# The mixing stage of a two-layer convolution kernel: another split of the nine depthwise taps over TensorE, VectorE and ScalarE, with the products in a ring of 7 slots

## The reference, cut to what matters

```python
# x: (8, 128, 256, 256) float32
def layer0(x):                                # x := x + this, of groupnorm(x)
    ll, lh, hl, hh = haar_dwt(x)              # four images of 128 x 128
    h = concat([ll, lh, hl, hh], axis=1)      # 512 channels
    h = gelu(batchnorm(conv1x1(h, w_c1, b_c1)))      # to 128 channels
    res = h
    o = dwconv3x3(h, dw_w, dw_b)              # nine taps for each channel
    o = layernorm_chw(o, gn_g, gn_b)          # one mean and variance for each image
    o = conv1x1(gelu(conv1x1(o, pw1_w, pw1_b)), pw2_w, pw2_b)
    h = o + res
    h = gelu(batchnorm(conv1x1(h, w_c2, b_c2)))      # to 512 channels
    return haar_idwt(h)
def layer1(x):                                # x := x + this, of groupnorm(x)
    return blur4x4(x)                         # the same 4 x 4 taps for all channels
```

## Time and profile before

| | |
|---|---|
| median of 3 runs | 5690.55 us (5673.53 to 5690.85) |
| the profiled execution's own time | 5687.8 us |
| its span | 5685.9 us |
| busy over the span: PE, DVE, ACT, POOL | 92%, 77%, 65%, 36% |
| mixing stage in the span | about 1236 to 2583 us |
| granted TensorE clock, mean over the span | 0.968 |

### The profile page before, as it was taken

One profiled execution on the slowest core, in us unless ns is written; L12 is line 12 of the kernel. 1 busy time (PEld: TensorE's weight loads), 2 busy tenths in 40 slices (PEclk: granted clock), 3 DMA queues, 4 the chain that ended last, 5 costly groups with the idle time before them and its releaser, 6 DMA issues. The chain is left out here.

```text
span 5685.9 us, 67157 instructions
## 1 busy us (share of the span) xinstructions
PE 5206.1 (92%) x18136; PEld 3152.4 (55%) x18136; DVE 4380.2 (77%) x5325; ACT 3721.4 (65%) x5012; POOL 2068.4 (36%) x1397
## 2 busy tenths in 40 slices
PE   2888888986999999996689999999999999999999
PEld 1333333332555555563256666666666766666677
DVE  8555555428999999957988888888888888888833
ACT  0333333346778777754678788787887877878744
POOL 0000000028777777730023333333333333333354
PEclk9999999998999999998899999999999999999999
DMA  9999999842333333326999999999999999999986
GB/s 368 374 372 380 369 380 378 345 143 71 108 108 112 104 108 108 108 83 226 326 381 403 393 401 398 390 402 384 398 392 384 394 384 397 399 384 395 400 292 228
DMA packets 829594, 1729.83 MB, mean 304 GB/s; under 512 B 50064, under 2 KB 587152, under 8 KB 718608
## 3 DMA queue, kind: packets, MB, share of 16 engines
q1 hardware_dynamic: 755472, 1389.81, 66.9%
q10 hardware_dynamic: 73728, 335.58, 14.4%
HBM read 1050.95 MB, written 674.23 MB: 303 GB/s over the span
## 5 line engine op out<-in xcount | busy, mean ns | idle before, releaser
L1080 POOL TENSOR_TENSOR y_lo<-y_centred_tile,y_hi 128x1024 fp32r<-128x1024 f32 x512 | 1042.3, 2057 | 1728.4 <-ACT y_centred_tile L1416 1422.9
L1295 PE MATMUL blur_psum<-y_hi,band_hi 128*128 128x512 f32 x4096 | 1129.3, 417 | 8.9 <-DVE y_tile L1173 7.4
L1278 PE MATMUL conv_psum<-u_in,w_conv 128*128 128x512 f32 x2048 | 975.3, 620 | 106.2 <-DVE pair_sums L1151 81.2
L1295 PE MATMUL blur_psum<-y_lo,band_hi 128*128 128x512 f32 x4096 | 1041.8, 396 | 6.7 <-POOL y_lo L1080 6.3
L1295 PEld LDWEIGHTS blur_psum<-y_hi,band_hi 128*128 128x128 f32 x4096 | 765.8, 188 | 278.8 <-issue 100.6
L1151 DVE TENSOR_TENSOR pair_sums<-gelu_out,conv_psum 128x512 f32<-128x512 f32 x1024 | 653.1, 683 | 308.7 <-ACT conv_psum L1386 308.6
L1295 PEld LDWEIGHTS blur_psum<-y_lo,band_hi 128*128 128x128 f32 x4096 | 769.7, 188 | 199.4 <-POOL y_lo L1080 14.8
L1173 DVE SCALAR_TENSOR_TENSOR y_tile<-blur_psum,rstd_all,y_tile 128x1024 f32<-128x1024 f32 x512 | 639.4, 1276 | 160.5 <-PE blur_psum L1295 153.1
L1386 ACT ACTIVATE gelu_out<-conv_psum,bn_shift,bn_scale 128x512 f32<-128x512 f32 x512 | 397.5, 776 | 534.1 <-PE conv_psum L1278 512.7
L1278 PEld LDWEIGHTS conv_psum<-u_in,w_conv 128*128 128x128 f32 x2048 | 399.4, 198 | 559.7 <-issue 406.2
L601 POOL TENSOR_TENSOR tap_products<-tap_products 128x512 f32<-128x512 f32 x512 | 653.5, 1276 | 42.7 <-ACT tap_products L838 6.2
(11 more groups left out here) (168 smaller groups left out, 5445.2 us busy)
## 6 DMA issues: line engine op xcount, KB each, us to landing
x_tile<-x SPq DMA_DIRECT2D x256, 1024.0 KB, 10.1
y_scratch<-x_tile ACTq DMA_DIRECT2D x256, 1024.0 KB, 8.4
y_tile<-y_scratch SPq DMA_DIRECT2D x512, 512.0 KB, 10.9
out<-y_tile SPq DMA_DIRECT2D x512, 512.0 KB, 10.4
x_stream<-x SPq DMA_DIRECT2D x192, 1024.0 KB, 11.6
x_resident<-x SPq DMA_DIRECT2D x160, 1024.0 KB, 11.0
z_scratch<-z_tile ACTq DMA_DIRECT2D x256, 256.0 KB, 7.2
z_in<-z_scratch SPq DMA_DIRECT2D x256, 256.0 KB, 3.6
```

Source lines behind the costliest of these rows:

```text
L1080: nc.gpsimd.tensor_tensor(y_lo[:, h, part, 2:2 + W], y_c[:, part, :], y_hi[:, h, part, 2:2 + W].bitcast(F32), ALU.subtract).then_inc(s_lo, 1)
L1278: nc.tensor.matmul(cv[s][:], w[:, s * C:(s + 1) * C], u_t[:, k % US, :], start=True, stop=True).then_inc(s_mm, 1)
L1295: ins = nc.tensor.matmul(bl[t][:, 2 * c:2 * c + 2, :], wt[:, kw, :], y[:, h, ch:ch + 2, kw:kw + W], start=(m == 0 and kw == 0), stop=(m == ...
```

## The change

The split of the nine taps now depends on the group. `split_of(e)` gives (PE, DVE, ACT): 4, 3, 2 for the 36 groups whose taps are computed while rows only enter (e < 36), and after that 2, 4, 3 for even and 1, 4, 4 for odd groups. Since the counts of signals for each group now differ, running totals (`DVE_BEFORE`, `ACT_BEFORE`, `ADD_BEFORE`) take the place of products like `(e + 1) * DVE_TAPS`. The products lie in one ring of 7 slots in place of two sets of 3; ACT waits before each product for what last read its slot: for a group's first product the final sum (`s_oo`), for the others an addition (`s_add`). In the steady steps two neighbouring groups have 7 products together, so product n of group e has the slot of product n of group e-2. PE's weight matrices are built for 4 taps, not 2. Queue orders, DMAs and all other buffers stay.

```diff
--- before.py
+++ after.py
@@ -414,9 +414,10 @@
 R2 = BANK // W2
 STEPS = H2 // R2
 ALL2 = B * STEPS
-PE_TAPS = 2
-ACT_TAPS = 3
-DVE_TAPS = TAPS - PE_TAPS - ACT_TAPS
+ENTER_TAPS = (4, 3, 2)
+STEADY_TAPS = ((2, 4, 3), (1, 4, 4))
+PE_MOST = 4
+PR_SLOTS = 7
 
 
 
@@ -424,6 +425,13 @@
 LEAVE = STEPS + BEHIND
 BLOCKS = STEPS + 1 + BEHIND + 1
 O_SLOTS = STEPS + BEHIND - 3
+
+
+
+def split_of(e):
+
+    return ENTER_TAPS if e < LEAVE - LAG_DW else STEADY_TAPS[e % 2]
+
 
 LAG_Z = 1
 LAG_TR = 1
@@ -435,6 +443,15 @@
 LAG_STATS = 5
 AHEAD = 2
 
+DVE_BEFORE = [0]
+ACT_BEFORE = [0]
+ADD_BEFORE = [0]
+for step in range(ALL2):
+    DVE_BEFORE.append(DVE_BEFORE[-1] + split_of(step)[1])
+    ACT_BEFORE.append(ACT_BEFORE[-1] + split_of(step)[2])
+    ADD_BEFORE.append(ADD_BEFORE[-1] + split_of(step)[2] - 1)
+PRODUCTS = [(e, n) for e in range(ALL2) for n in range(split_of(e)[2])]
+
 
 def phase_mix(nc, kp, pw1, pw2, const, z_d, u_d):
     K, V, n128, neg_half = kp["K"], kp["V"], kp["n128"], kp["neg_half"]
@@ -447,12 +464,12 @@
         plane = sb("h_ring", [128, 4 * BLOCKS + 2, W2 + 2])
         o_buf = sb("depthwise_out", [128, O_SLOTS, BANK])
         z_in = sb("z_in", [128, 4, BANK])
-        diag = sb("tap_diagonals", [128, PE_TAPS, C])
+        diag = sb("tap_diagonals", [128, PE_MOST, C])
         w1 = sb("pw1_weights", [128, C])
         w1f = sb("pw1_folded", [128, 2, C])
         w2 = sb("pw2_weights", [128, C])
         v_t = sb("gelu1_out", [128, 2, BANK])
-        products = sb("tap_products", [128, 2, ACT_TAPS, BANK])
+        products = sb("tap_products", [128, PR_SLOTS, BANK])
         u_t = sb("u_tile", [128, 4, BANK])
         u_tr = sb("u_transposed", [128, 2, 4, C + 1])
         bst = sb("o_stats", [128, STEPS, BN_W])
@@ -593,16 +610,17 @@
                     nc.gpsimd.tensor_tensor(t[:, 3:4], t[:, 2:3], neg_half[:, 0:1], ALU.pow).then_inc(s_rs, 1)
                 if e == ALL2:
                     break
-                pr = products[:, e % 2]
-                for n in range(1, ACT_TAPS):
-                    pool.wait_ge(s_pr, e * ACT_TAPS + n + 1)
+                first = products[:, ACT_BEFORE[e] % PR_SLOTS, :]
+                for n in range(1, split_of(e)[2]):
+                    pool.wait_ge(s_pr, ACT_BEFORE[e] + n + 1)
                     if n > 1:
-                        pool.wait_ge(s_add, e * (ACT_TAPS - 1) + n - 1)
-                    nc.gpsimd.tensor_tensor(pr[:, 0, :], pr[:, 0, :], pr[:, n, :], ALU.add).then_inc(s_add, 1)
-                pool.wait_ge(s_add, (e + 1) * (ACT_TAPS - 1))
-                pool.wait_ge(s_lk_tap, (e + 1) * DVE_TAPS)
+                        pool.wait_ge(s_add, ADD_BEFORE[e] + n - 1)
+                    nc.gpsimd.tensor_tensor(first, first, products[:, (ACT_BEFORE[e] + n) % PR_SLOTS, :],
+                                            ALU.add).then_inc(s_add, 1)
+                pool.wait_ge(s_add, ADD_BEFORE[e + 1])
+                pool.wait_ge(s_lk_tap, DVE_BEFORE[e + 1])
                 o = o_buf[:, e % O_SLOTS, :]
-                nc.gpsimd.tensor_tensor(o, o, pr[:, 0, :], ALU.add).then_inc(s_oo, 1)
+                nc.gpsimd.tensor_tensor(o, o, first, ALU.add).then_inc(s_oo, 1)
 
         @block.vector
         def _(dve):
@@ -624,7 +642,7 @@
             nc.vector.scalar_tensor_tensor(bn1_d[:], t[:, 6:7], bn1_a[:], V[:, V_BN1B:V_BN1B + 1],
                                            ALU.mult, ALU.add).then_inc(s_bn1, 1)
             dve.wait_ge(s_id, 16)
-            for k in range(PE_TAPS):
+            for k in range(PE_MOST):
                 nc.vector.tensor_scalar(diag[:, k, :], K[:, K_ID:K_ID + C], V[:, V_DWW + k:V_DWW + k + 1],
                                         None, ALU.mult).then_inc(s_bn1, 1)
             taps = Chain(dve, s_lk_tap)
@@ -645,8 +663,9 @@
                 if e >= O_SLOTS:
                     dve.wait_ge(s_p1, e - O_SLOTS + 1)
                 acc = dw_p[e % 2][:]
-                for n, k in enumerate(range(PE_TAPS, PE_TAPS + DVE_TAPS)):
-                    to = o_buf[:, e % O_SLOTS, :] if n == DVE_TAPS - 1 else acc
+                on_pe, on_dve, _ = split_of(e)
+                for n, k in enumerate(range(on_pe, on_pe + on_dve)):
+                    to = o_buf[:, e % O_SLOTS, :] if n == on_dve - 1 else acc
                     taps.link(nc.vector.scalar_tensor_tensor(
                         to.rearrange("p (r c) -> p r c", c=W2), tap(k, e),
                         V[:, V_DWW + k:V_DWW + k + 1],
@@ -717,7 +736,7 @@
 
         @block.tensor
         def _(pe):
-            pe.wait_ge(s_bn1, 1 + PE_TAPS)
+            pe.wait_ge(s_bn1, 1 + PE_MOST)
             pe.wait_ge(s_zero, 5)
 
             def taps_step(e):
@@ -725,10 +744,11 @@
                 wait_rows(pe, e)
 
                 if e >= 2:
-                    pe.wait_ge(s_lk_tap, (e - 1) * DVE_TAPS)
-                for k in range(PE_TAPS):
+                    pe.wait_ge(s_lk_tap, DVE_BEFORE[e - 1])
+                count = split_of(e)[0]
+                for k in range(count):
                     ins = nc.tensor.matmul(dw_p[e % 2][:], diag[:, k, :], tap(k, e),
-                                           start=(k == 0), stop=(k == PE_TAPS - 1))
+                                           start=(k == 0), stop=(k == count - 1))
                 ins.then_inc(s_dw, 1)
 
             def pw2_step(l):
@@ -831,11 +851,17 @@
 
                 wait_rows(act, e)
 
-                if e >= 2:
-                    act.wait_ge(s_oo, e - 1)
-                for n in range(ACT_TAPS):
-                    k = TAPS - ACT_TAPS + n
-                    nc.scalar.activation(products[:, e % 2, n, :].rearrange("p (r c) -> p r c", c=W2), tap(k, e),
+                for n in range(split_of(e)[2]):
+                    i = ACT_BEFORE[e] + n
+                    if i >= PR_SLOTS:
+
+                        e0, n0 = PRODUCTS[i - PR_SLOTS]
+                        if n0 == 0:
+                            act.wait_ge(s_oo, e0 + 1)
+                        else:
+                            act.wait_ge(s_add, ADD_BEFORE[e0] + n0)
+                    k = TAPS - split_of(e)[2] + n
+                    nc.scalar.activation(products[:, i % PR_SLOTS, :].rearrange("p (r c) -> p r c", c=W2), tap(k, e),
                                          ACT.Copy, scale=V[:, V_DWW + k:V_DWW + k + 1]).then_inc(s_pr, 1)
 
             for p in range(LAG_Z, ALL2 + LEAVE + LAG_EVAC):
```

## The result

The changed kernel takes 5709.85 us (median of 7 runs, 5706.39 to 5717.06) against 5690.55 us before (7 runs, 5673.53 to 5697.34). The ratio is 1.0043, with a 95% interval from 1.0031 to 1.0054: 18 to 31 us slower. Forecast was 5713 us. In the profiled executions the span grew from 5685.9 to 5712.5 us, by 26.6 us.

The account below looks back on a forecast made before the run. Before, POOL bounds entering steps (4.00 us) and PE steady ones (4.77 us); after, PE and a four-step loop of waits. -15.7 + 41 - 4 + 4 = +25.3 us on 5687.8 gives 5713 us; 8 in 10: 5683 to 5742.

Parts of the forecast that it names:

- Entering steps, -15.7 us: While rows only enter: PE becomes the bound at 3.44 us a step instead of 4.01, net 15.7 us less.
- The start at 1.2 GHz: Mixing stage's start: first eight matmuls at 1.2 GHz now serve one group, first final sum 2.0 us later.
- Steady steps, +41 us: Steps after filling: 4.96 us each against 4.77, 0.19 us more over some 216 steps, +41 us.
- The loop: Steady steps: longest chain of waits through POOL, ACT, PE and DVE, odd group to odd group, 19.83 us for four steps.
- the pieces: Nine start-to-start times from an odd group's final sum to the one four steps later, summing to 19.83 us.
- Seams, -4 and +4 us: Between images, seven times: -4 us as the norm chain bounds three steps, +4 us as busier POOL stretches DVE's small instructions.
- Sum: Whole kernel: entering steps, steady steps and seams together +25.3 us on 5687.8 us, 5713 us.
- The two-step loop (no change): Steady steps: chain through one product set of odd groups bounds at 9.65 us, 4.83 a step, total 5685 us; chance 0.12.
- POOL alone (faster): Steady steps: POOL's own work of 9.41 us for two groups bounds, 4.71 a step, total 5659 us; chance 0.08.
- DVE's sum of 9.04 us: Steady steps: DVE's own work over two neighbouring groups with four taps in both, 2 x (4.77 - 0.25) us.
- PE's clock (slower): Odd steady steps at 1.2 GHz, 3.9 us longer each; six such events give 5736 us; chance 0.08.

Follow-up runs that it names:

- the entering half alone: Against the kernel before: 4, 3, 2 while rows only enter, 2, 4, 3 in all steady steps, ring of 6; 5663.58 us, ratio 0.9951.

## Why the prediction was right

- *Entering steps, -15.7 us.* The final sum of group 31 starts at 1358.75 where it started at 1373.42; with the stage's start 0.8 us later that is -15.5 us. The first image's statistics come only 13.5 us sooner, because DVE reaches `statistics(31)` behind `depthwise(32)`, which now waits for PE; that I had not counted. The start at 1.2 GHz (granted clock 0.50 from 1243.1 to 1246.3) and the full clock behind it (1.00 from 1249.9 to 1253.0) were as assumed. The start varies, though: in the run with the entering half alone the clock is 1.00 from 1243.5 us on, 3.2 us behind the first matmul, where the changed kernel needed some 6.8, and its first final sum comes 1.8 us sooner after the stage's start.
- *Steady steps, +41 us.* The loop was forecast at 19.83 us and measured at 19.84, in a pattern of four steps. Each of the pieces read from the rows held: final sum to product 1.37, four products 2.46, GELU to matmul 0.73, PE step 4.86, residual 1.07, first tap 0.66, four taps 3.26, first addition 1.23, three additions 4.19 (1641.12 to 1645.31). Seven images at +6.1 us are +42.7.
- *Seams, -4 and +4 us.* A seam costs 4.6 us before and after, so this was right in total, but the +4 us had the wrong reason. The fold was stretched in six of eight images already before (8.1 us for the eight, 9.4 after), so it added 1.3 us and not 4. What the sum left out is the clock in a seam. Ten microseconds around the end of a seam's long step, first before, then after:

```profile
1698.00:1708.00 10.00, 8.62 (x37) 5.20 (x38) 9.49 (x15) 6.59 (x11) 6.29 (x6) 1.00 0.30 98
...
1699.00:1709.00 10.00, 9.75 (x38) 5.92 (x39) 8.70 (x14) 7.66 (x12) 6.93 (x7) 0.83 0.29 100
```

  Of the six seams from the second to the seventh it is down in two before (0.78 and 0.83, long steps of 11.12 and 9.65 us; the other four 1.00 and 7.95 us) and in five after (0.83, 8.93 to 9.28 us; the sixth 1.00 and 7.27). In the two seams shown PE had waited 2.7 us for the folded weights before and 3.2 after. The length of this wait alone does not tell when the clock falls: before, it had waited 2.7 us too in the two seams where it fell, and after, it had waited 2.9 us both in a seam where it fell (1535 us) and in the one where it did not (2353 us). The six long steps add up to 52.6 us before and 52.3 after: that they cancel is luck.
- *Sum.* Forecast +25.3 us, profiled span +26.6, by the ratio +24.5. The stage alone is +29.0; the other stages, 2.4 us shorter by scatter, brought the span nearer to the forecast.
- *The two-step loop (no change)* is refuted by the pattern of four steps and by the odd split 2, 3, 4, whose steps stayed at 19.83 us for four with DVE's 0.79 us taken out of it.
- *POOL alone (faster)* was the highest of the engines' own sums and appeared to the hundredth, 4.71 us, as soon as the first product's wait was gone. In the change as made the wait hid it. DVE's sum of 9.04 us was too high: with two steps of 4.41 it is 8.8; the forecast did not rest on it.
- *PE's clock (slower)* came in five seams, as said, and not in the steps between: the steps shown keep the lengths of the loop, and the window of 200 us, with one seam in it, has 0.99. The seams together cost no more than before, so it did not show in the time.

## What to carry to other kernels

Sums of busy time for each engine say what a split of work could give; whether it gives it is decided by the longest closed loop of waits through all queues, and that can span several steps when steps alternate. In a pipeline near balance, write that loop out with start-to-start times from one traced step: here it came out right to 0.01 us for two loops (19.84 for 19.83 us, 14.44 for 14.44) and to 0.06 for a third (19.15 for 19.21). A buffer that collects a sum should be the one read last, not the first: the same instructions with the sum rolled into the later slot gave the early slot back at once, and turned a loss of 0.4% into a gain of 0.6%, or of 1.0% with a split that fits the sums. A step less one wait is only an upper bound of an engine's own sum, since other idle time may hide in it: by that DVE had 4.52 us a step, in fact 4.41.

## What of the hardware I had not expected

The clock in a seam was not in the sum of the prediction: around the end of the long step it is 0.83 over ten microseconds in five seams of six, where before it was 1.00 in four of six; PE had waited 2.9 us in one of the five (1535 us) and 2.7 us in the one shown before, where it stayed at 1.00.

Two more were in the prediction and are seen again. A pointwise matmul that had to wait for its input lasts 1.12 or 1.13 for 1.02 us, and the next step is 4.87 us long, not 4.77: 0.10 us, needed once on the loop to hit its 19.83 us. And DVE's fold of the weights (0.29 us) took 1.26 us in the first seam too, now that a final sum of POOL ran beside it, as in the second seam before:

```profile
1367.93 1.26 POOL L623 TENSOR_TENSOR depthwise_out<-depthwise_out,tap_products 128x512 f32<-128x512 f32 x1 [0.71 <-DVE depthwise_out L669]
1368.01 1.26 DVE L702 TENSOR_SCALAR pw_folded<-pw_weights,small_columns 128x128 f32<-128x128 f32 x1
```
